# Two-layer gated cross-attention kernel: narrower top-k pieces, guard rows sent ahead of two key loads, and the second attention's first keys and queries loaded in the phase before

## The chip, the cores and the metric

One core of a Trainium2 chip runs the whole program in one launch. The metric is device time in microseconds of that core. The median of three runs of the kernel before is 3328.2 us (3325.5 to 3335.14).

## What is computed

The reference is a two-layer block over x (16 sequences of 256 tokens, 128 wide) and a context (16 x 1601 tokens, 96 wide), in float32:

```
x = x + tanh(g_xattn[0]) * L0_xattn(ln(x), ctx)   # 4 heads; top 32 of 1601 scores, softmax over them,
                                                  # mean over heads; FiLM, a long convolution, an MLP, a layer norm
x = x + tanh(g_ffn[0])   * L0_ffn(ln(x))          # 8 experts, one per token, at most 512 tokens each
x = x + tanh(g_xattn[1]) * L1_xattn(ln(x), ctx)
x = x + tanh(g_ffn[1])   * L1_ffn(ln(x))          # 8 experts, one per token, hidden 512

L1_xattn(x, c):  q = x @ w_q + b_q;  k = c @ w_k + b_k;  v = c @ w_v + b_v   # 16 heads of 8
                 w = softmax(q k^T / sqrt(8));  return (w v) @ w_o + b_o
```

The first attention needs, for each of 16 x 4 x 256 = 16384 score rows of 1601 values, the 32 largest.

## The kernel before

The program is a row of phases, each a block in which every engine has its own instruction stream and waits on semaphores. A block ends when all engines have ended it.

**First attention** (`attention0_phase`, about 190 to 1400 us). It walks 16 batches of 8 score tiles (4 heads x 2 halves of 128 rows). TensorE makes a tile of 128x1601 scores, ScalarE copies it to SBUF (`sc`, L870), VectorE finds the 32nd largest of each row, ScalarE and GpSimd turn that into masked exponentials (L877, L617, L883), VectorE adds tiles in pairs (L1044), TensorE multiplies them on. VectorE's search cuts a row into pieces of `PICK` = 51 columns (32 pieces), takes the eight largest of each (`MAX8`, L986), and then searches the 32 x 8 = 256 candidates with four `MAX8` (L1020) and three `MATCH_REPLACE8` (L1022). The first pass of the next tile is woven in: two pieces ahead of each step of the second search. If a row has more than eight of its top 32 in one piece, the candidates are not enough. ScalarE and TensorE count for each tile the values above the found threshold (`side`, `dps`, `doubts`); VectorE reads the count (`settle`, L974) and, where it is too high, searches the whole tile again with `select_all` (L961): four times `MAX8` and `MATCH_REPLACE8` over 1601 columns, and three passes more. ScalarE's exponential of that tile waits for `settled`.

**Convolution** (`conv_phase`), which also splits the keys of batches 0 and 1 into three bf16 parts (`keys` in DRAM), and the **middle phase** (`middle_phase`, 1485 to 1804 us): MLP, the first experts, and the queries of the second attention, split into three bf16 parts and saved by SyncE in 24 DMAs (L1322), three for each group of two batches. SyncE's order there is: eight loads of `FO` (from the third on each after `x_ready` of the group two before), 39 stores of a blank row block into `sorted` (L1318), the 24 saves. `x_ready` of a group says that `FO`, `Y` and `X0` of it have been read.

**Second attention** (`attention1_phase`, 1804 to about 3090 us). Scores must carry float32 precision through bf16 products, so rows of `ks` and `qs` hold seven pairs of parts (`PAIRS`, 7 x 8 = 56 rows) for even heads and, 64 rows further, for odd heads; three rows more, the guard rows, hold ones in `ks` and the parts of minus the row maximum in `qs`, so that a 59-row product (L1974) gives score minus maximum. Before them go 56-row products (L1949) of which VectorE takes only maxima (L2056). `ks[i]`, `qs[i]` and `va[i]` exist twice; batch b uses number b % 2.

At its start VectorE sets both `ks` to 1.0 (L2048) and adds the output bias to `X` (L2050, L2051); GpSimd sets both `qs` and both `va` to 0 (L1818, L1821). SyncE loads keys and queries of batches 0 and 1 only after that (`ready`, `ks_ready`), 28 DMAs per group of four heads. Then comes a prologue: maxima for batch 0 and the first head group of batch 1, 80 pieces of work; then 16 batches.

A batch has four head groups, a group 13 key tiles (`kt`). At each key tile TensorE does the scores of four heads, a product for maxima of the batch ahead, and the products with the values for the tile two before (L1987: four heads, each into its own 32 of the 128 output partitions, since `va` has `VW` = 32 columns per head, of which 9 carry something); ScalarE does the exponentials (L2030). In the last group, at the sixth and seventh key tile, TensorE turns the parts of the maxima (`guard`, L1953), VectorE copies them to `mT` (L2074), and SyncE sends `mT` to DRAM (L1901), waits for it, and loads it into the guard rows of the other `qs` (L1906). The first scores of the next batch wait for `guard_in`. Maxima run one batch ahead, those of the first head group two.

SyncE's order in the second attention (`batch(b)`, L1916) is what the change touches:

```
for g in range(HG - 1): load(b + 2, par, g, True)      # groups 0, 1, 2; each waits for pv_done of group g of batch b
load_values(b + 2, True)
guard(b + 1, 1 - par, ...)                             # waits for mT_ready
load(b + 2, par, HG - 1, True)                         # group 3
```

Each `load` is 14 DMAs of keys (L1887) and 14 of queries (L1888). The maxima of (b + 2, group 2) are due at group 1 of batch b + 1, those of group 3 at group 2. GpSimd meanwhile spreads the values into `va` (L1834) and splits later batches' keys (L1839 on).

**Second experts** (`mixture1_phase`), untouched.

Of the kernel before, what the change touches and what calls it, by code (L numbers as in the profile page):

```python
# [15 lines left out]
P = 128  # L16
# [15 lines left out]
BIG = 1e30  # L32
HIDDEN = 2.0 ** 45
# [3 lines left out]
PICK = 51  # L37
# [1164 lines left out]
def middle_phase(nc, a, k):  # L1202
# [3 lines left out]
    with ExitStack() as ctx:  # L1206
# [32 lines left out]
        blank = sb("m_blank", [P, ROW])  # L1239

# [60 lines left out]
        dve_step, pool_step, blank_ready, blanked = sem("m_dve_step"), sem("m_pool_step"), sem("m_blank_ready"), sem("m_blanked")  # L1301
        block = ctx.enter_context(nc.Block())

        @block.sync
        def _(sp):
            for name, t in (("g_ffn", gcol), ("b_ffn", bcol)):
                sp.dma_start(t[:, :], a["L0_xattn_" + name].unsqueeze(1)).then_inc(w_in, 16)
            for g in range(NG):
# [4 lines left out]
                if g == 1:  # L1313
                    for name, t in rowsb.items():
                        sp.dma_start(t[:, :], a["L0_xattn_" + name].partition_broadcast(P)).then_inc(rows_in, 16)
            sp.wait_ge(blank_ready, 1)
# [12 lines left out]
        def _(pool):  # L1329
# [3 lines left out]
            def constants():  # L1333
# [10 lines left out]
                pool.sem_inc(consts, 1)  # L1344
                st.link(g_.memset(blank[:, :], 0.0))
# [305 lines left out]
def attention1_phase(nc, a, k):  # L1651
# [8 lines left out]
    PAIRS = [(0, 0), (1, 0), (2, 0), (0, 1), (1, 1), (2, 1), (0, 2)]  # L1660
    ROWS = 64
    GUARD = DH1 * len(PAIRS)
# [7 lines left out]
    with ExitStack() as ctx:  # L1670
# [6 lines left out]
        ks = [sb(f"ks{i}", [P, H1 // 2, NK], BF16) for i in range(2)]  # L1677
        qs = [sb(f"qs{i}", [P, H1, S], BF16) for i in range(2)]
        vn = sb("vn", [P, KT, D])
        kfb = sb("kfb", [P, NK])  # L1680
        kpb = [sb(f"kpb{n}", [P, NK], BF16) for n in range(3)]
        va = [sb(f"va{i}", [P, KT, H1, VW]) for i in range(2)]
# [15 lines left out]
        ready, vn_in, va_ready = sem("a_ready"), sem("vn_in"), sem("va_ready")  # L1698
# [5 lines left out]
        pe_passed, pool_passed, ks_ready = sem("a_pe_passed"), sem("a_pool_passed"), sem("ks_ready")  # L1704
# [106 lines left out]
        def _(pool):  # L1811
# [13 lines left out]
            st.restart()  # L1825

# [30 lines left out]
            spread_values(1, 1)  # L1857
            for b in (2, 3):
                split_keys(b)
# [10 lines left out]
        def _(sp):  # L1870
# [3 lines left out]
            def load(b, par, g, started):  # L1874

                if started:
# [673 lines left out]
```

## Time and profile before

| | |
|---|---|
| profiled execution, its own time | 3325.87 us |
| its span, first to last instruction | 3324.4 us |
| median of three runs | 3328.2 us |
| TensorE busy (matmul) | 2556.5 us, 77% |
| VectorE busy | 2380.3 us, 72% |
| ScalarE busy | 2055.0 us, 62% |
| GpSimd busy | 1246.9 us, 38% |
| mean granted TensorE clock | 0.879 |
| L2056 maxima, VectorE, x1024 | 957.4 us, 988 ns each |
| L2030 exponentials, ScalarE, x1664 | 896.6 us |
| L986 pieces' `MAX8`, VectorE, x4096 | 562.9 us, 197 ns each |
| L1987 value products, TensorE, x6656 | 555.8 us, 407 ns each |

Busy time of a group counts overlap once, so a mean times a count can be more than it. Four products of L1987 into four output quarters overlap. A clock of 1.0 is 2.4 GHz, 0.5 is 1.2 GHz. A bracket behind an instruction in a timeline is the idle time of its engine before it, with what ended it.

### The profile page before, as it was taken

The page shows a single profiled execution, that of the slowest core. Times are in us where ns is not written, and L with a number is a line of the kernel's source. Part 1 is how long each engine was busy: PE and PEld are TensorE (multiplying, and loading weights), DVE is VectorE, ACT ScalarE, POOL GpSimd, SP SyncE. Part 2 cuts the span into 40 slices and gives each one's busy share as a digit, 9 for nine tenths or more (in the row PEclk, how much of TensorE's full clock was granted, in tenths as well). Part 3 has the DMA queues.
Part 4 walks back from the last instruction along what each step waited for, and adds up shares of the span by engine and source line. Part 5 has one row for each costly group of instructions (what it writes and reads, how often), then busy time and mean ns, then how long its engine had stood idle before and what let it go on. Part 6 is the DMA issues. An engine that isn't in the chain of part 4 may idle for free. (4 is left out here: it accounts for less than half of the span.)

```text
span 3324.4 us, 68050 instructions
## 1 busy us (share of the span) xinstructions
PE 2556.5 (77%) x19550; PEld 1303.9 (39%) x19550; DVE 2380.3 (72%) x7659; ACT 2055.0 (62%) x3368; POOL 1246.9 (38%) x1587
## 2 busy tenths in 40 slices
PE   1058888888678888758784589898989889999468
PEld 0035555555445555535321133333333333333335
DVE  5948887787887878636545988888888878883312
ACT  1148888888668888615221077777777777779112
POOL 2037766777557767613102032221111112100332
PEclk9978988898888888889787589999999999999679
DMA  2010010001001001083001633232322323220221
GB/s 54 0 31 32 32 42 33 31 31 50 30 18 46 31 31 42 26 274 95 1 18 29 102 97 89 86 90 81 84 82 84 85 87 85 81 53 2 71 77 45
DMA packets 136744, 195.94 MB, mean 59 GB/s; under 512 B 51842, under 2 KB 104511, under 8 KB 136363
## 3 DMA queue, kind: packets, MB, share of 16 engines
q1 hardware_dynamic: 126350, 152.17, 16.8%
q0 software_dynamic: 10016, 39.46, 3.3%
q8 instruction: 148, 2.42, 0.3%
q14 instruction: 230, 1.88, 0.2%
HBM read 125.38 MB, written 66.62 MB: 58 GB/s over the span
## 5 line engine op out<-in xcount | busy, mean ns | idle before, releaser
L2030 ACT ACTIVATE pb<-sps 128x512 f32<-128x512 f32 (+1 forms) x1664 | 896.6, 596 | 377.3 <-PE sps L1974 363.1
L2056 DVE TENSOR_REDUCE mx<-wps 128x2 f32<-128x802 f32 x1024 | 957.4, 988 | 157.0 <-PE wps L1949 140.7
L986 DVE MAX8 cand<-sc 128x8 f32<-128x51 f32 (+1 forms) x4096 | 562.9, 197 | 193.8 <-issue 162.0
L1987 PE MATMUL ops<-pb,va 128*32 128x256 f32 x6656 | 555.8, 407 | 7.6 <-ACT ot L2036 7.2
L749 PE MATMUL scores<-ctxT,qT 97*128 97x512 f32 (+1 forms) x1024 | 437.6, 576 | 43.8 <-ACT sc L870 42.7
L1949 PE MATMUL wps<-ks,qs 56*128 56x401 bf16 x2048 | 384.7, 361 | 105.1 <-DVE mx L2056 53.2
L1974 PE MATMUL sps<-qs,ks 59*128 59x256 bf16 (+1 forms) x3328 | 363.5, 284 | 70.3 <-DMA qs<-guards 69.8
L1834 POOL COPY va<-vn 128x128 f32<-128x128 f32 (+1 forms) x208 | 49.9, 292 | 796.6 <-PE ops L1987 720.0
L749 PEld LDWEIGHTS scores<-ctxT,qT 97*128 97x128 f32 x1024 | 210.5, 215 | 274.9 <-issue 220.6
L1974 PEld LDWEIGHTS sps<-qs,ks 59*128 59x128 bf16 (+1 forms) x3328 | 120.7, 96 | 411.0 <-ACT pb L2030 242.2
L617 POOL TENSOR_TENSOR prf<-sc,prf 128x1601 f32<-128x1601 f32 x64 | 230.0, 3594 | 119.0 <-ACT prf L877 118.1
L617 POOL TENSOR_TENSOR prs<-sc,prs 128x1601 f32<-128x1601 f32 x64 | 230.8, 3607 | 94.8 <-ACT prs L877 94.8
L1987 PEld LDWEIGHTS ops<-pb,va 128*32 128x32 f32 x6656 | 133.5, 110 | 213.1 <-issue 108.6
L723 PE MATMUL misc<-diag,prs 128*128 128x128 f32 (+1 forms) x1664 | 203.1, 280 | 9.3 <-DVE prs L1044 4.7
L891 ACT ACTIVATE side<-sc,below 128x1601 bf16<-128x1601 f32 x128 | 207.3, 1620 | 1.7 <-POOL below L611 1.7
L1949 PEld LDWEIGHTS wps<-ks,qs 56*128 56x128 bf16 x2048 | 110.6, 97 | 240.9 <-DVE mx L2056 165.3
L723 PEld LDWEIGHTS misc<-diag,prs 128*128 128x128 f32 (+1 forms) x1664 | 192.8, 191 | 11.1 <-DVE prs L1044 6.3
L870 ACT COPY sc<-scores 128x1601 f32<-128x1601 f32 x128 | 188.4, 1472 | 11.8 <-PE scores L749 11.8
L1020 DVE MAX8 top<-cleft 128x8 f32<-128x256 f32 x384 | 157.5, 410 | 0.1
L732 PE MATMUL misc<-prT,ctxn 128*96 128x128 f32 (+1 forms) x832 | 117.7, 308 | 45.7 <-ACT prT L851 45.7
L611 POOL TENSOR_SCALAR below<-slack,top 128x1 f32<-128x1 f32 x128 | 140.7, 1099 | 13.0
L732 PEld LDWEIGHTS misc<-prT,ctxn 128*96 128x96 f32 (+1 forms) x832 | 110.7, 189 | 52.5 <-ACT prT L851 52.5
(408 smaller groups left out, 3697.1 us busy)
## 6 DMA issues: line engine op xcount, KB each, us to landing
ks<-keys SPq DMA_DIRECT2D x896, 50.0 KB
keys<-kpb POOLq DMA_DIRECT2D x42, 400.2 KB, 3.3
toep<-kernpad SPq DMA_DIRECT2D x8, 2048.0 KB, 15.0
qs<-queries SPq DMA_DIRECT2D x896, 8.0 KB
values<-vs SPq DMA_DIRECT2D x16, 832.0 KB, 3.7
vn<-values SPq DMA_DIRECT2D x16, 832.0 KB, 4.7
keysf<-kf SPq DMA_DIRECT2D x16, 800.5 KB, 4.6
kfb<-keysf POOLq DMA_DIRECT2D x14, 800.5 KB, 5.5
```

The costliest lines, as they stand in the source:

```text
L617: g.tensor_tensor(pr[s][:, :], sc[s % 4][:, :], pr[s][:, :], ALU.subtract).then_inc(kept_ready, 1)
L723: ins = t.matmul(m[0:kn(kt), (kt % 4) * P:(kt % 4) * P + P], pr[s][:, kt * P:kt * P + kn(kt)], diag[s // 2][:, :], start=(p == 0), stop=(p ...
L732: ins = t.matmul(m[0:C, 0:P], ctxn[par][0:kn(kt), kt, :], prT[0:kn(kt), kt, :], start=(kt == 0), stop=(kt == KT - 1))
L749: ins = t.matmul(scores[:, c:c + n], q, ctxT[par][0:C + 1, c:c + n], start=True, stop=True)
L870: s_.copy(sc[s % 4][:, :], scores[:, 0:NK]).then_inc(scores_out, 1)
L891: s_.activation(side[s % 2][:, :], sc[s % 4][:, :], ACT.Sign, bias=below32[:, s % 2:s % 2 + 1], accum_out=sides[:, s % 2:s % 2 + 1]).then_ ...
L986: st.add(v.max(cand[s % 2][:, n, :], sc[s % 4][:, c:c + w]))
L1949: ins = t.matmul(buf[:, 512 * odd:512 * odd + WIN], qs[par][r, h + odd, q * P:q * P + P], ks[par][r, h // 2, (WIN - 1) * c:(WIN - 1) * c + ...
L1974: ins = t.matmul(sps[(UNITS * g + u) % SB][0:kn(kt), i, :], ks[par][r, h // 2, kt * P:kt * P + kn(kt)], qs[par][r, h, :], start=True, stop ...
L1987: ins = t.matmul(ops[VW * i:VW * i + VW, 0:S], va[par][0:kn(kt), kt, 4 * g + i, :], pb[(UNITS * g + 2 * kt + i % 2) % 8][0:kn(kt), i // 2, :],
L2030: nc.scalar.activation(pb[(UNITS * g + u) % 8][0:rows_, :, :], sps[(UNITS * g + u) % SB][0:rows_, :, :], ACT.Exp).then_inc(p_ready, 1)
L2056: v.tensor_reduce(mx4[:, q, h:h + 2, c], both, AX.X, ALU.max).then_inc(work_read, 1)
```

## The change

- `PICK` goes from 51 to 46: 35 pieces instead of 32, 280 candidates instead of 256.
- `PAIRS`, `ROWS`, `GUARD` move to the top of the file.
- `ks`, `qs`, `kfb`, `vn` of the second attention are no tensors of their own any more: they lie over `FO`, `X0` with `XF` (now one tensor), and `Y`, and so exist in the middle phase.
- SyncE loads all keys and all queries of batches 0 and 1 in the middle phase: keys and guard rows of ones in 32 DMAs after the last `x_ready`, ahead of the blank stores; queries in 28 DMAs after the second group's saves. The block ends only when they have landed.
- GpSimd sets a small tensor of ones (3 x 1601) for the guard rows. The whole memsets of `ks`, `qs` and `va` go; `va` has 9 columns per head and only its ninth is set.
- VectorE clears the PSUM bank `ops` once. The bias is added to `X` by GpSimd, after it spread the values of batches 0 and 1; VectorE's first guard copy waits for it.
- SyncE's order in a batch becomes: groups 0 and 1, values, guard, groups 2 and 3.

```diff
-PICK = 51
+PICK = 46
@@ middle_phase, sync
                 if g == 1:
                     for name, t in rowsb.items():
                         sp.dma_start(t[:, :], ...).then_inc(rows_in, 16)
+            sp.wait_ge(x_ready, NG)
+            sp.wait_ge(ones_ready, 1)
+            for b in range(2):
+                for odd in range(2):
+                    for i, (_, kp) in enumerate(PAIRS):
+                        r = slice(ROWS * odd + DH1 * i, ROWS * odd + DH1 * (i + 1))
+                        sp.dma_start(k.ks[b][r, :, :], kall[b, odd, kp]).then_inc(keys_in, 16)
+                    r = ROWS * odd + GUARD
+                    sp.dma_start(k.ks[b][r:r + 3, :, :], ones3[:, :].unsqueeze(1).to_broadcast([3, H1 // 2, NK])
+                                 ).then_inc(keys_in, 16)
             sp.wait_ge(blank_ready, 1)
...
             for g in range(NG):
                 sp.wait_ge(parts_ready, g + 1)
...
+                if g == 1:
+                    sp.wait_ge(saved[0], 48)
+                    for b in range(2):
+                        for odd in range(2):
+                            for i, (qp, _) in enumerate(PAIRS):
+                                r = slice(ROWS * odd + DH1 * i, ROWS * odd + DH1 * (i + 1))
+                                sp.dma_start(k.qs[b][r, odd:H1:2, :], qall[odd, qp, :, :, b * S:(b + 1) * S]
+                                             ).then_inc(queries_in, 16)
...
+            sp.wait_ge(keys_in, 16 * 2 * 2 * (len(PAIRS) + 1))
+            sp.wait_ge(queries_in, 16 * 2 * 2 * len(PAIRS))
@@ attention1_phase
-        va = [sb(f"va{i}", [P, KT, H1, VW]) for i in range(2)]
+        va = [sb(f"va{i}", [P, KT, H1, DH1 + 1]) for i in range(2)]
@@ gpsimd
-            for i in range(2):
-                st.link(g_.memset(qs[i][:, :, :], 0.0))
-                pool.sem_inc(ready, 1)
-            for i in range(2):
-                st.add(g_.memset(va[i][:, :, :, :], 0.0))
-            st.after()
...
             spread_values(0, 0)
             spread_values(1, 1)
+            st.link(g_.tensor_scalar(k.bo1[:, :], k.bo1[:, :], k.TG[:, 1:2], 0.0, ALU.mult, ALU.add))
+            st.link(g_.tensor_tensor(X[:, :, :], X[:, :, :], rows(k.bo1[:, :], T), ALU.add))
+            pool.sem_inc(biased, 1)
@@ sync
             for b in range(2):
-                sp.wait_ge(ready, b + 1)
-                sp.wait_ge(ks_ready, b + 1)
-                for g in range(HG):
-                    load(b, b, g, False)
                 load_values(b, b == 1)
             guard(0, 0, False)
 
             def batch(b, par):
 
-                for g in range(HG - 1):
-                    load(b + 2, par, g, True)
+                for g in range(HG - 2):
+                    load(b + 2, par, g)
                 load_values(b + 2, True)
                 guard(b + 1, 1 - par, not (isinstance(b, int) and b == 0))
-                load(b + 2, par, HG - 1, True)
+                for g in range(HG - 2, HG):
+                    load(b + 2, par, g)
@@ tensor, maxima
-                if opens:
-                    pe.wait_ge(kq_in[par][h // 4], 16 * 2 * 2 * len(PAIRS) * visit)
+                if opens and not (isinstance(visit, int) and visit == 1):
+                    pe.wait_ge(kq_in[par][h // 4], 16 * 2 * 2 * len(PAIRS) * (visit - 1))
@@ tensor, values
-                    ins = t.matmul(ops[VW * i:VW * i + VW, 0:S], va[par][0:kn(kt), kt, 4 * g + i, :],
+                    ins = t.matmul(ops[VW * i:VW * i + DH1 + 1, 0:S], va[par][0:kn(kt), kt, 4 * g + i, :],
@@ vector
-            for i in range(2):
-                st.link(v.memset(ks[i][:, :, :], 1.0))
-                dve.sem_inc(ks_ready, 1)
-            st.link(v.tensor_scalar(k.bo1[:, :], k.bo1[:, :], k.TG[:, 1:2], None, ALU.mult))
-            st.link(v.tensor_tensor(X[:, :, :], X[:, :, :], rows(k.bo1[:, :], T), ALU.add))
+            st.link(v.memset(ops[:, :], 0.0))
+            dve.sem_inc(ops_blank, 1)
```

## Rows read from the trace of the kernel before

**Rows 1.** Waits of the whole span: engine line <- releaser: us in total, times, longest.

```profile
PE sps L1974 <- DMA qs<-guards: 69.8, 15, 6.6
```

**Rows 2.** Timeline of a batch's end: VectorE, SyncE's queue, TensorE.

```profile
2424.85 0.20 DVE L2074 COPY mT<-wps 48x128 bf16<-48x128 bf16 x1
...
2416.88 0.28 SPq L1887 DMA_DIRECT2D ks<-keys  x1
...
2428.85 0.28 SPq L1888 DMA_DIRECT2D qs<-queries  x1
2429.31 0.36 SPq L1893 DMA_DIRECT2D vn<-values  x1
2429.88 0.34 SPq L1901 DMA_DIRECT2D guards<-mT  x1
2435.22 0.58 SPq L1906 DMA_DIRECT2D qs<-guards  x2
...
2437.78 0.61 PE L1974 MATMUL sps<-qs,ks 59*128 59x256 bf16 x4 [5.71 <-DMA qs<-guards]
```

**Rows 3.** Timeline of the last batch boundary, and the windows row of that stretch.

```profile
3024.87 0.22 DVE L2074 COPY mT<-wps 48x128 bf16<-48x128 bf16 x1 [0.84 <-PE wps L1958]
...
3026.74 0.57 SPq L1906 DMA_DIRECT2D qs<-guards  x2
...
3030.86 0.27 PE L1974 MATMUL sps<-qs,ks 59*128 59x256 bf16 x1
...
3000.00:3050.00 50.00, 48.37 (x580) 17.46 (x572) 20.99 (x32) 46.16 (x92) 0.00 (x0) 1.00 0.01 3
```

**Rows 4.** Windows of L1987 on TensorE (busy, count, clock), then of all TensorE.

```profile
2388.00:2401.00 13.00, 7.03 (x88) 1.00 0.31 88
...
2437.70:2444.40 6.70, 3.35 (x28) 0.51 0.08 20
...
1982.90:2964.40 981.50, 881.87 (x9984) 0.94 0.30 84
```

**Rows 5.** Windows: stretch, length, busy PE, PEld, DVE, ACT, POOL; PEclk, DMA share, GB/s.

```profile
400.00:700.00 300.00, 254.24 (x1310) 171.28 (x1309) 242.66 (x1466) 253.73 (x349) 213.93 (x265) 0.90 0.10 35
```

**Rows 6.** Timeline of the second attention's start.

```profile
1806.56 10.73 DVE L2048 MEMSET ks<- 128x12808 bf16 x1 [6.14 <-issue]
...
1835.80 14.49 DVE L2056 TENSOR_REDUCE mx<-wps 128x2 f32<-128x802 f32 x16
```

**Rows 7.** Middle phase: line 1371's instructions; SyncE's queue.

```profile
L1371 DVE TENSOR_TENSOR xt<-xt,X x8: 691/693/693, 1492.2 to 1584.1; 128x512 f32<-128x512 f32 x8
...
1556.95 20.36 SPq L1318 DMA_DIRECT2D sorted<-m_blank  x39
1683.29 118.53 SPq L1322 DMA_DIRECT2D queries<-q_p  x24
```

**Rows 8.** Instructions of line 1135, products with 16 columns of weights.

```profile
L1135 PE MATMUL cv<-toep,xc x256: 376/379/634, 1433.8 to 1481.2; 128*16 128x256 f32 x128
```

**Rows 9.** Instructions of line 968: durations ns min/median/max, first and last start.

```profile
L968 DVE MAX8 top<-sc x8: 1829/1829/1830, 837.4 to 963.6; 128x8 f32<-128x1601 f32 x8
```

**Rows 10.** Timeline of GpSimd at three batch starts (start us, duration us, engine, line).

```profile
566.24 0.40 POOL L591 COPY xn<-X 128x256 f32 x1
...
781.17 0.40 POOL L591 COPY xn<-X 128x256 f32 x1
...
1029.60 0.40 POOL L591 COPY xn<-X 128x256 f32 x1
```

**Rows 11.** Timeline of VectorE in one tile's search.

```profile
718.62 0.41 DVE L1020 MAX8 top<-cleft 128x8 f32<-128x256 f32 x1
718.95 2.10 DVE L986 MAX8 cand<-sc 128x8 f32<-128x51 f32 x18
```

**Rows 12.** Timeline where ScalarE follows GpSimd's threshold most closely.

```profile
665.25 0.19 POOL L601 TENSOR_SCALAR negm<-top 128x1 f32<-128x1 f32 x1
...
666.57 1.63 ACT L877 ACTIVATE prf<-sc,cutoff 128x1601 f32<-128x1601 f32 x1
```

More of the change, by code:

```diff
@@ L32 @@
 BIG = 1e30
+PAIRS = [(0, 0), (1, 0), (2, 0), (0, 1), (1, 1), (2, 1), (0, 2)]
+ROWS = 64
+GUARD = DH1 * len(PAIRS)
 HIDDEN = 2.0 ** 45
@@ L1315, in _ @@
                         sp.dma_start(t[:, :], a["L0_xattn_" + name].partition_broadcast(P)).then_inc(rows_in, 16)
+            sp.wait_ge(x_ready, NG)
+            sp.wait_ge(ones_ready, 1)
+            kall = k.keys.rearrange("b n (pr o d) c -> b o n d pr c", o=2, d=DH1)
+            qall = k.queries.rearrange("n (pr o d) c -> o n d pr c", o=2, d=DH1)
+            for b in range(2):
[6 more added lines that the diff above has]
+                                 ).then_inc(keys_in, 16)
             sp.wait_ge(blank_ready, 1)
@@ L1344, in constants @@
                 pool.sem_inc(consts, 1)
+                st.link(g_.memset(ones3[:, :], 1.0))
+                pool.sem_inc(ones_ready, 1)
                 st.link(g_.memset(blank[:, :], 0.0))
@@ L1675, in sem @@
             return ctx.enter_context(nc.semaphore(name))
[L1677 to L1680, printed above, removed]
+        ks, qs, vn, kfb = k.ks, k.qs, k.vn, k.kfb
         kpb = [sb(f"kpb{n}", [P, NK], BF16) for n in range(3)]
-        va = [sb(f"va{i}", [P, KT, H1, VW]) for i in range(2)]
+        va = [sb(f"va{i}", [P, KT, H1, DH1 + 1]) for i in range(2)]
         pb = [sb(f"pb{i}", [P, 2, S]) for i in range(8)]
@@ L1696, in attention1_phase @@
         X, ident = k.X, k.ident
-        ready, vn_in, va_ready = sem("a_ready"), sem("vn_in"), sem("va_ready")
+        vn_in, va_ready, ops_blank, biased = sem("vn_in"), sem("va_ready"), sem("ops_blank"), sem("a_biased")
         kq_in = [[sem(f"kq_in{i}{g}") for g in range(HG)] for i in range(2)]
@@ L1872, in _, with load @@
             qall = k.queries.rearrange("n (pr o d) c -> o n d pr c", o=2, d=DH1)
[L1874 to L1880 removed]
+            def load(b, par, g):
+                sp.wait_ge(pv_done, KT * (HG * (b - 2) + g + 1))
+                sp.sem_inc(sp_passed, 1)
+                sp.wait_ge(k.keys_out, 48 * (b - 1))
+                sp.sem_inc(sp_passed, 1)
                 pr = slice(2 * g, 2 * g + 2)
@@ L1955, in guard @@
                 pe.wait_ge(mparts_ready, b + 1)
+                if isinstance(b, int) and b == 0:
+                    pe.wait_ge(identb_ready, 1)
                 work(job)
@@ L1984, in values @@
                     pe.wait_ge(ops_read, HG * b + g)
+                if kt == 0 and first and g == 0:
+                    pe.wait_ge(ops_blank, 1)
                 pe.wait_ge(p_ready, UNITS * HG * b + UNITS * g + 2 * kt + 2)
                 for i in range(4):
-                    ins = t.matmul(ops[VW * i:VW * i + VW, 0:S], va[par][0:kn(kt), kt, 4 * g + i, :],
+                    ins = t.matmul(ops[VW * i:VW * i + DH1 + 1, 0:S], va[par][0:kn(kt), kt, 4 * g + i, :],
                                    pb[(UNITS * g + 2 * kt + i % 2) % 8][0:kn(kt), i // 2, :],
@@ L2073, in guard @@
                     dve.wait_ge(mT_saved, 16 * b)
+                if isinstance(b, int) and b == 0 and q == 0:
+                    dve.wait_ge(biased, 1)
                 st.link(v.tensor_copy(mT[:, q, :], buf[0:3 * H1, 0:P // 2].bitcast(BF16)))
@@ L2521, in flamingo_kernel @@
                 conv_phase(nc, a, k)
+                flat = [t.rearrange("p a d -> p (a d)") for t in
+                        (k.FO[:, :, :], XX[:, :, :, :].rearrange("p i t d -> p (i t) d"), k.Y[:, :, :])]
+                words = H1 // 2 * NK // 2
+                k.ks = [t[:, 0:words].bitcast(BF16).rearrange("p (r c) -> p r c", c=NK) for t in flat[0:2]]
+                k.kfb = flat[0][:, words:words + NK]
+                k.vn = flat[1][:, words:words + KT * D].rearrange("p (t d) -> p t d", d=D)
+                k.qs = [flat[2][:, i * H1 * S // 2:(i + 1) * H1 * S // 2].bitcast(BF16).rearrange("p (h c) -> p h c", c=S)
+                        for i in range(2)]
                 middle_phase(nc, a, k)
-        attention1_phase(nc, a, k)
+                attention1_phase(nc, a, k)
         mixture1_phase(nc, a, k)
```

17 lines of the change are left out of this document (7 added, 10 removed).

## The prediction

> **What bounds the kernel now.** I read the waits of the whole run first, then the timelines at two kinds of batch boundary of the second attention, the windows with the granted clock, and last the first attention's tiles. The profiled execution took 3325.87 us, 2.3 below the median of 3328.2; the sum is made against the 3325.9.
>
> The second attention runs on TensorE and VectorE together (88 value products in 13 us are 11 key tiles at 8 a tile, 1.18 us each and 15.4 us for a group of 13 [rows 4]), except at its batch boundaries: there TensorE waits for the guard rows, 15 times, 69.8 us in all [rows 1]. One boundary shows why [rows 2]. VectorE has `mT` ready at 2425.05. SyncE is then still issuing the 28 loads of group 2 (2416.88 to 2429.13), issues 832 KB of values, sends `mT` only at 2429.88, has it back at 2435.22 and loads the guard rows; TensorE starts at 2437.78 after 5.71 us idle, so it wanted them at 2432.07. At the last boundary no loads are left [rows 3]: `mT` ready at 3025.09, second DMA at 3026.74, TensorE goes on at 3030.86 with no wait at all and the clock stays at full speed (1.00).
>
> The wait costs more than itself. After it, TensorE's granted clock is 0.51 for 6.7 us, the lower level of 1.2 GHz; before, it was 1.00 [rows 4]. In the low stretch 28 value products start in 6.7 us (4.18 per us) against 88 in 13 us (6.77 per us): 38% of that time is lost. Over 13 batches the mean clock is 0.94, so 12% of 981.5 us, 118 us, are at the low level.
>
> The first attention is ScalarE's: 253.7 us busy in 300, VectorE 242.7 [rows 5]. VectorE has some slack there, except where a tile is searched again.
>
> **The change part by part.**
>
> *Guards ahead of groups 2 and 3.* SyncE is free from group 1's loads on. At the last boundary it needs 1.65 us from `mT` ready to the guard DMA [rows 3]; the guard load itself takes 2.56 us (2435.22 to 2437.78, [rows 2]). So the guard rows are there at 2425.05 + 1.65 + 2.56 = 2429.3, 2.8 us before they are wanted. The values load is now ahead of the guard by 11 us and has landed. The first of the 15 waits, 4.5 us, is the prologue's and stays; it has no loads ahead of it. The other 14 go: 69.8 - 4.5 = 65.3 us. What is late next: nothing at TensorE's order; VectorE has 64 maxima a batch of 957.4/1024 = 0.935 us busy (line 2056 in the table), 60 us, and a few us of small work, while the batch falls from 75.5 (981.5/13) to about 68 us. It is the next bound, but not yet reached.
>
> *The low clock after it.* At 14 boundaries the low stretch ends 6.4 to 9.3 us after the wait does, by the granted clock, 7.6 in the mean; 14 x 7.6 x 0.38 = 40.6, 41 us. One of them stands in [rows 4], and [rows 3] has the boundary without a wait and without a fall. Bounds: 0, if the small products at a batch's start make the fall, to 118 x 0.5 = 59 us. I take 41.
>
> The Trainium skill gives another price for such a stretch (TensorE: Matmul & The Clock Gate, section Terms): the time at the lower level times the share of pulses taken away, so a half here. By that the 118 us would cost 59 and the sum would come out 18 us lower (rival 6). The row does not agree, 38% and not 50% [rows 4].
>
> *Keys of groups 2 and 3 later.* Group 2's loads start after the guard's, at 2427.3 instead of 2416.88, need 12.3 us to issue [rows 2] and end at 2439.6; group 3's follow to 2452. TensorE needs group 2 one group into the next batch, 2432 + 15.4 and some 3 us of the last batch's output work, 2450.5, and group 3 at 2466. With a few us to land (the 832 KB, the guard and back took 8 us together in [rows 2]) some 5 us are left for the first and more for the second. Cost 0; above it, see the slow rival.
>
> *The start.* Today the first maxima reduction is at 1835.80 [rows 6], behind 10.7 us of memset, 15 us of loads and the bias on `X`. Now VectorE begins at 1806.56 as before with a PSUM memset of 512 columns (the memset of 12808 bf16 columns took 10.73 us, so under 1 us), and everything else is in place: 1807.3. Gain 28.5 us, all on the path, since the 80 pieces of the prologue follow one another on VectorE. GpSimd's bias add and its spreading have until the first guard copy, 80 x 14.49/16 = 72.5 us later: hidden. Bounds 25 to 31.
>
> *Middle phase.* `x_ready` of the last group comes at about 1585 [rows 7]. The loads of [rows 2] brought 0.8 MB in 13 us, 62 GB/s with the issuing engine as the limit; 5.7 MB of keys take at most 92 us, to 1677; the blank stores, 20 us by their row, then end at 1697, at worst 14 us after the first query save was due (1683.29). The eight groups' saves come 118.5/7 = 16.9 us apart and each buffer is wanted again only two groups later, 34 us, so this is hidden; the queries' 28 loads (0.9 MB) fall into the gap after group 1. Cost 0, at worst 10 us at the end of the block. GpSimd's small memset lies beside TensorE's first MLP group: 0, at most its own us or two.
>
> *Nine columns.* Value products with 16 columns of weights and 256 moving take 379 ns and also four at a time [rows 8], those with 32 columns 403: no change, bounds -10 to +10 us.
>
> *Pieces.* The eight `MAX8` of 1601 columns [rows 9] mean that two tiles were searched again. Their price is in [rows 10]: three batches from 566.24 to 781.17 take 214.9 us, the three with the two tiles (to 1029.60) 248.4; 33.5 us for two. Which rows have more than eight of their top 32 in one piece can be counted from the reference's inputs (seed 0): with pieces of 51, one row in each of two tiles (batch 8, head 0 and batch 9, head 3), which agrees with the rows' place in the trace; with 46, none. So 33.5 us go. Against it: 18 `MAX8` of 51 take 2.10 us, 117 ns each [rows 11]. From 256 to 1601 columns `MAX8` grows by 1.055 ns a column (410 to 1829 ns), so one of 46 takes 111.5: 35 x 111.5 - 32 x 117 = 160 ns. The second search has seven steps over 24 columns more, 177 ns. Together 0.34 us a tile, 43 us of VectorE for 128 tiles. Where ScalarE comes closest behind, it takes the tile 1.1 us after GpSimd's threshold [rows 12]; the threshold itself moves by 0.1 us in its own tile (16 shorter pieces lie ahead of it), and VectorE is idle 57 us in 300 [rows 5], 1.7 us a tile (a batch of 8 tiles takes 71.6) against 0.34 added, so the lag stays under that 1.1. Cost 0; if the cover is gone, 43.
>
> **Sum.** 3325.9 - 65.3 - 41 - 28.5 - 33.5 = 3157.6; I say 3158.
>
> **The rivals.**
> 1. The low clock stays at the boundaries. For it: in some of the 14 the fall begins only as the wait ends, and the short transposing products come there anyway. Against: [rows 3]. 3158 + 41 = 3199.
> 2. Pieces exposed: VectorE becomes the first attention's bound. For: 81% busy; against: it idles while ScalarE works. 3158 + 43 = 3201.
> 3. Guards are still late by half. For: 2.8 us of margin rests on one undisturbed trip; against: nothing else is in the queue. 14 x 2.3 = 32, and the low clock with it: 3158 + 32 + 41 = 3231.
> 4. Slower: the keys come late. Where groups 2 and 3 together miss their group, TensorE waits in every batch at the place where it has no wait today. The margin is about 5 us; each us past it costs 14. The gain of 168 us is used up at 12 us of waiting a batch, 17 us later than reckoned. For: both loads are now back to back, 24 us of issue, beside 2 MB of GpSimd's. With 14 us a batch, 3158 + 196 = 3354.
> 5. The change doesn't do what it says: the start is not earlier, because SyncE's new work ends the middle phase later. 3158 + 28 = 3186.
> 6. The low clock costs half of all its time, 118 x 0.5 = 59 us instead of 41. For: whatever stands behind TensorE slows with it; against: 38% by the counts of [rows 4], VectorE's reduction does not slow with TensorE, and some of the low time lies inside waits that are counted already. 3158 - 18 = 3140. (The skill's price above.)
>
> **How the numbers follow.** The forecast has 0.62 (its own range 3142 to 3180), rival 1 0.12, rival 2 0.06, rival 3 0.07, rival 4 0.03, rival 5 0.04, rival 6 0.06. The range 3132 to 3210 takes in rivals 1, 2, 5 and 6 and leaves out 3 and 4. What a measurement of this kernel can tell from no change is 0.3%, 10 us: faster 0.96, same 0.01, slower 0.03.
>
> **What would show it.** Right: no wait of `sps` for `qs<-guards` but the first; the batches' mean clock near 1.0 with 68 us a batch; first reduction at 1807; no `MAX8` over 1601 columns; the first attention ending some 33 us earlier. Wrong: waits of `wps` for `ks` or `qs` at groups 1 and 2; ScalarE waiting for GpSimd's threshold; a middle phase that ends later than 1804 less those 33.

## The result, and the profile after

The kernel after takes 3189.53 us (median of four runs, 3186.89 to 3194.58), the kernel before, in the same comparison, 3331.67 (3325.5 to 3337.04). The ratio is 0.9576, 95% interval 0.9553 to 0.9598. That is inside the predicted range and 31 us above the 3158 forecast. The profiled execution took 3194.58 us, 131.3 less than the one before. By stages, from the starts and ends of the tiles named, in us of the two profiled executions:

| stage | before | after | difference | forecast |
|---|---|---|---|---|
| to the first score copy `sc` | 207.9 | 210.4 | +2.5 | 0 |
| first attention, to the last `side` | 1186.9 | 1155.7 | -31.2 | -33.5 |
| convolution and middle phase, to the first maxima reduction | 441.0 | 408.8 | -32.2 | -28.5 |
| prologue of the second attention | 79.3 | 78.9 | -0.3 | 0 |
| its 16 batches, first to last exponential | 1171.6 | 1101.3 | -70.3 | -106.3 |
| the rest | 237.7 | 238.0 | +0.3 | 0 |

So 36 of the missing 37 us are missing in the 16 batches. The page of the kernel after: busy times, the granted clock by slices, and the groups that answer to the table of before (`maxima` is now line 2078, the exponentials line 2055, the value products line 2012, the pieces line 990).

```profile
PE 2533.8 (79%) x19550; PEld 1274.0 (40%) x19550; DVE 2360.1 (74%) x8010; ACT 2050.6 (64%) x3368; POOL 1241.8 (39%) x1586
...
PEclk9978988989999899778878589999999999999589
...
L2055 ACT ACTIVATE pb<-sps 128x512 f32<-128x512 f32 (+1 forms) x1664 | 894.0, 596 | 282.5 <-PE sps L1997 268.8
L2078 DVE TENSOR_REDUCE mx<-wps 128x2 f32<-128x802 f32 x1024 | 954.1, 989 | 93.1 <-PE wps L1970 77.7
L990 DVE MAX8 cand<-sc 128x8 f32<-128x46 f32 (+1 forms) x4480 | 587.0, 194 | 164.8 <-issue 128.6
L2012 PE MATMUL ops<-pb,va 128*9 128x256 f32 x6656 | 527.2, 389 | 9.4 <-ACT ot L2061 8.4
```

**The waits that answer to [rows 1]**, second attention of the kernel after (us in all, times, longest):

```profile
PE sps L1997 <- issue: 19.8, 5, 4.3
PE sps L1997 <- DMA Y<-guards: 4.0, 1, 4.0
```

The guard waits are gone but for the prologue's. In their place stand five pauses for which the view names no releaser ("issue": the engine waited for nothing that the profile shows). They come at the ends of batches 2, 4, 6, 8 and 10 and nowhere else. The timeline of one of them answers to [rows 2]; the bracket is TensorE's idle time:

```profile
2189.75 0.21 DVE L2098 COPY mT<-wps 48x128 bf16<-48x128 bf16 x1
...
2190.14 0.34 SPq L1924 DMA_DIRECT2D guards<-mT  x1
2191.58 0.59 SPq L1929 DMA_DIRECT2D Y<-guards  x2
2192.94 0.29 SPq L1910 DMA_DIRECT2D FO<-keys  x1
...
2200.93 0.61 PE L1997 MATMUL sps<-Y,XX 59*128 59x256 bf16 x4 [4.01 <-issue]
```

and the same place one batch earlier, where SyncE issues the same loads, TensorE does not stop and the scores follow 5.3 us behind the guard load. Above, 5.3 us behind it is 2196.9, which is where TensorE's idle time begins:

```profile
2120.79 0.21 DVE L2098 COPY mT<-wps 48x128 bf16<-48x128 bf16 x1
2121.18 0.34 SPq L1924 DMA_DIRECT2D guards<-mT  x1
...
2122.62 0.59 SPq L1929 DMA_DIRECT2D Y<-guards  x2
...
2127.89 0.60 PE L1997 MATMUL sps<-Y,FO 59*128 59x256 bf16 x4
```

What differs is the code. Batches 1 to 12 are a loop of six passes of two batches (`walk`, line 1822 after, 1797 before), so behind batches 2, 4, 6, 8 and 10 TensorE, ScalarE and VectorE jump back (SyncE and GpSimd have loops of their own); behind batch 12 they fall through, and there is no pause. The trace has the loop's own instructions, seen by their line: kind, number, shortest, median and longest in ns, first and last start. "PEldq" is TensorE's sequencer. Kernel after, then the kernel before:

```profile
L1822 ACTq COMPARE_BRANCH  x6: 40/45/50, 2051.7 to 2769.8; - x6
L1822 PEldq COMPARE_BRANCH  x6: 83/4331/4737, 2051.7 to 2769.8; - x6
```

```profile
L1797 PEldq COMPARE_BRANCH  x6: 83/5870/6167, 2127.7 to 2885.5; - x6
```

A jump back of TensorE takes 4.0 to 4.7 us (the five single records), the last one, not taken, 83 ns. Before, it took 5.5 to 6.2 us and lay in the same stretch as the guard wait: at the boundary of [rows 2] it ran from 2431.3 to 2437.1, while the guard rows came at 2437.8. The cover was the wait that the change removes.

**Clock and pace of the batches**, windows of the kernel after: all of value products in a full-speed stretch and in the stretch behind a jump (they answer to [rows 4]), then batches 1 to 12 whole. Columns as in [rows 5]; the first two rows are of line 2012 alone.

```profile
2388.00:2401.00 13.00, 6.46 (x88) 1.19 (x80) 1.00 0.38 118
2344.90:2351.60 6.70, 3.42 (x28) 0.50 (x32) 0.50 0.27 72
```

```profile
1917.80:2771.00 853.20, 796.47 (x9218) 269.58 (x9216) 754.79 (x913) 682.29 (x1296) 197.28 (x264) 0.96 0.33 91
```

88 products in 13 us and 28 in 6.7, as before: the low level costs the same 38%. Batches 1 to 12 take 71.1 us each (853.2/12), not 68, at a clock of 0.96; low stretches within the batches fell from 137 to 69 us. Of the 69, 51 are five stretches of 10.2 us at the jumps, 4 lie in batch 0, and 14 are four short ones of 3.4 us (from 2182.2, 2325.5, 2544.0 and 2755.6), 15 to 20 us ahead of a batch's end. Two of these four ends, those of batches 9 and 12, have no jump.

**Start of the second attention** (answers to [rows 6]) and the middle phase (to [rows 7]: instructions of line 1402, which was 1371, then SyncE's queue):

```profile
1774.16 0.48 DVE L2072 MEMSET ops<- 128x512 f32 x1 [3.62 <-PEq L1210]
...
1774.79 2.79 DVE L2078 TENSOR_REDUCE mx<-wps 128x2 f32<-128x802 f32 x3
```

```profile
L1402 DVE TENSOR_TENSOR xt<-xt,XX x8: 691/691/694, 1462.5 to 1554.4; 128x512 f32<-128x512 f32 x8
```

```profile
1593.86 16.73 SPq L1331 DMA_DIRECT2D XX<-keys  x7
1610.63 1.83 SPq L1333 DMA_DIRECT2D XX<-m_ones  x1
1612.51 33.48 SPq L1337 DMA_DIRECT2D sorted<-m_blank  x39
1653.57 21.21 SPq L1341 DMA_DIRECT2D queries<-q_p  x6
1674.82 9.76 SPq L1349 DMA_DIRECT2D Y<-queries  x28
1693.44 78.49 SPq L1341 DMA_DIRECT2D queries<-q_p  x18
```

**First attention** (answers to [rows 10]); three batches now take 215.0 and 212.6 us:

```profile
573.04 0.40 POOL L595 COPY xn<-XX 128x256 f32 x1
...
788.01 0.40 POOL L595 COPY xn<-XX 128x256 f32 x1
...
1000.65 0.40 POOL L595 COPY xn<-XX 128x256 f32 x1
```

### The profile page after: what moved, and what is told of

Read it like the earlier page. It is cut to its first block and busy times, and to the rows that moved or that the text cites. A ratio compares the mean times of both kernels' runs of the same rounds, so it can differ in the third digit from the quotient of the medians.

```text
span 3193.1 us, 68227 instructions
## 1 busy us (share of the span) xinstructions
PE 2533.8 (79%) x19550; PEld 1274.0 (40%) x19550; DVE 2360.1 (74%) x8010; ACT 2050.6 (64%) x3368; POOL 1241.8 (39%) x1586
## 5 line engine op out<-in xcount | busy, mean ns | idle before, releaser
L990 DVE MAX8 cand<-sc 128x8 f32<-128x46 f32 (+1 forms) x4480 | 587.0, 194 | 164.8 <-issue 128.6
L2012 PE MATMUL ops<-pb,va 128*9 128x256 f32 x6656 | 527.2, 389 | 9.4 <-ACT ot L2061 8.4
L1854 POOL COPY va<-XX 128x128 f32<-128x128 f32 (+1 forms) x208 | 50.3, 295 | 706.4 <-PE ops L2012 698.7
L1970 PE MATMUL wps<-FO,Y 56*128 56x401 bf16 x1024 | 196.8, 368 | 49.4 <-DVE mx L2078 34.6
L1970 PE MATMUL wps<-XX,Y 56*128 56x401 bf16 x1024 | 186.6, 343 | 26.4 <-DVE mx L2078 18.1
L1997 PE MATMUL sps<-Y,XX 59*128 59x256 bf16 (+1 forms) x1664 | 184.9, 282 | 20.0 <-issue 19.8
L1997 PE MATMUL sps<-Y,FO 59*128 59x256 bf16 (+1 forms) x1664 | 180.3, 278 | 4.3 <-DMA Y<-guards 4.0
L2012 PEld LDWEIGHTS ops<-pb,va 128*9 128x9 f32 x6656 | 99.1, 88 | 208.2 <-issue 98.4
L1024 DVE MAX8 top<-cleft 128x8 f32<-128x280 f32 x384 | 167.7, 437 | 0.1
L1997 PEld LDWEIGHTS sps<-Y,XX 59*128 59x128 bf16 (+1 forms) x1664 | 63.1, 96 | 197.9 <-ACT pb L2055 124.5
## 6 DMA issues: line engine op xcount, KB each, us to landing
toep<-kernpad SPq DMA_DIRECT2D x8, 2048.0 KB, 14.9
```

What stands on the lines that cost most here:

```text
L990: st.add(v.max(cand[s % 2][:, n, :], sc[s % 4][:, c:c + w]))
L1024: link(v.max(tp[:, 8 * r:8 * r + 8], x))
L1970: ins = t.matmul(buf[:, 512 * odd:512 * odd + WIN], qs[par][r, h + odd, q * P:q * P + P], ks[par][r, h // 2, (WIN - 1) * c:(WIN - 1) * c + ...
L1997: ins = t.matmul(sps[(UNITS * g + u) % SB][0:kn(kt), i, :], ks[par][r, h // 2, kt * P:kt * P + kn(kt)], qs[par][r, h, :], start=True, stop ...
L2012: ins = t.matmul(ops[VW * i:VW * i + DH1 + 1, 0:S], va[par][0:kn(kt), kt, 4 * g + i, :], pb[(UNITS * g + 2 * kt + i % 2) % 8][0:kn(kt), i ...
```

## Experiments

Eleven kernels. The ratio of each is to the kernel before, timed beside it, with the 95% interval.

### The loop written out for three engines (`a_unroll`) and for TensorE alone (`a_unroll_pe`)

```diff
@@ attention1_phase, walk
-            with eng.Fori(0, (B - 4) // 2) as i:
+            for i in range((B - 4) // 2):
                 batch(2 * i + 1, 1, {1: i + 2, 2: i + 2}, False, 2)
                 batch(2 * i + 2, 0, {1: i + 2, 2: i + 3}, False, 2)
```

> The kernel after, with the second attention's loop over batches 1 to 12 (six passes of two batches) written out for TensorE, ScalarE and VectorE; SyncE and GpSimd keep their loops. Theory J (the jump back): at the ends of batches 2, 4, 6, 8 and 10 the engines jump back to the loop's start, and TensorE's branch takes 4.0 to 4.7 us there; that is what the pauses of 3.6 to 4.4 us before the first scores of batches 3, 5, 7, 9, 11 are (19.8 us), and the fall of the clock behind each (10.2 us of low level, 38% of it lost, 3.9 us each) comes from them. Written out: 5 x (4.0 + 3.9) = 39 us less, 3150 us, no pause at a batch boundary, batches of 68 us all through. Rival G (the guard rows are still late every second batch, because group 2's loads are issued right behind them): the pauses stay where they are, 3185 to 3190 us. Rival C (the clock falls at these places whatever TensorE waits for): the pauses go, the low stretches stay, 3170 us.

Measured: 3139.63 us, ratio 0.9427 (0.9389 to 0.9465), 50 us less than the kernel after. Waits of `sps` in the batches are gone, and every batch from 1 to 13 takes 66.43 or 66.44 us at full clock (the window is batches 1 to 12):

```profile
1926.30:2723.50 797.20, 756.11 (x9219) 252.73 (x9216) 750.32 (x913) 679.37 (x1296) 197.24 (x264) 1.00 0.35 97
```

Theory J holds, G and C fall: SyncE's order and its DMAs are the same, and in batches 1 to 15 neither pause nor low stretch is left. The gain is 11 us larger than expected. A batch inside the loop that neither jumps nor loses clock takes 67.61 us, written out 66.43: 1.18 us, 14 in twelve batches, and the expectation had the number and left it out of its sum. What differs in such a batch is the sequencers' register arithmetic for semaphore values: in batch 1 of the kernel after the trace has 177 `ALU_OP` on TensorE's sequencer, 153 on ScalarE's and 68 on VectorE's, and written out none.

> The kernel after, with the same loop written out for TensorE alone; ScalarE and VectorE still jump back. Between their last instruction before the jump and the first behind it ScalarE shows 3.6 us and VectorE 3.8 us too. Theory J with all engines alike: TensorE's pause goes, but ScalarE comes back only some 2.5 us after it would be wanted, so TensorE stands behind it for 1 to 2.5 us instead of 4: 5 x 1.5 to 3 us less and the clock partly held, 3170 to 3182 us. Rival T (only TensorE's jump matters, the others jump while they would idle anyway): as when all are written out, 3150 us. Rival G: 3185 to 3190 us.

Measured, with only `walk(pe, ...)` written out: 3171.79 us, ratio 0.9533 (0.9496 to 0.9569), 18 us less than the kernel after by the medians and 14 by the ratios, inside J's 3170 to 3182. The timeline at the end of batch 4: ScalarE and VectorE come 2 us late from their own jumps, and TensorE stands 1.3 us behind them.

```profile
2196.18 2.14 ACT L2060 ACTIVATE pb<-sps 128x512 f32<-128x512 f32 x4 [2.05 <-PE ops L2017]
...
2196.84 0.49 PE L2002 MATMUL sps<-Y,XX 59*128 59x256 bf16 x3 [1.32 <-ACT pb L2060]
2197.18 1.89 DVE L2083 TENSOR_REDUCE mx<-wps 128x2 f32<-128x802 f32 x2 [2.03 <-issue]
```

The five stops are 1.2 to 1.7 us long; after three of them the clock still fell, for 6.8 us each. Their branches read 45 and 63 ns, yet these engines pause too: the branch's own duration shows the cost on TensorE only. This run also says whose register arithmetic costs time. TensorE has none left here, and the undisturbed batches 9, 11 and 12 still take 67.75 us, so the 1.18 us belong to ScalarE's or VectorE's; which of the two was not tried.

### Two jumps instead of five (`a_double`)

```diff
-            with eng.Fori(0, (B - 4) // 2) as i:
-                batch(2 * i + 1, 1, {1: i + 2, 2: i + 2}, False, 2)
-                batch(2 * i + 2, 0, {1: i + 2, 2: i + 3}, False, 2)
+            with eng.Fori(0, (B - 4) // 4) as i:
+                for j in range(2):
+                    batch(4 * i + 2 * j + 1, 1, {1: 2 * i + j + 2, 2: 2 * i + j + 2}, False, 2)
+                    batch(4 * i + 2 * j + 2, 0, {1: 2 * i + j + 2, 2: 2 * i + j + 3}, False, 2)
```

> The kernel after with the second attention's loop of six passes of two batches turned into three passes of four: two jumps back instead of five, all in the same loop arithmetic on registers. It parts the 50 us that writing the loop out brought (3139.6 against 3189.5) into jumps and registers. Theory J: a jump costs 4.0 us of pause and 3.9 of clock, and the registers' part, 1.2 us a batch (67.6 us for a batch in the loop at full clock, 66.4 for one written out), stays: 3 x 7.9 = 24 us less, 3166 us, pauses only at the ends of batches 4 and 8. Rival R: the gain was the registers', the pauses are covered elsewhere: 3185 to 3190 us. Rival L: a longer body makes a jump dearer, 10 us and more each, since more must be fetched: 3175 to 3185 us.

Measured: 3168.44 us, ratio 0.9520 (0.9488 to 0.9551), 21 us less than the kernel after by the medians, 19 by the ratios. The waits of `sps` and the branch:

```profile
PE sps L1998 <- issue: 6.2, 2, 3.1
```

```profile
L1822 PEldq COMPARE_BRANCH  x3: 83/3577/3583, 2191.4 to 2745.8; - x3
```

Batches 1 to 12 take 826.2 us. Twelve at 67.61 would be 811.3, so 14.9 us are above that here, and 42 in the kernel after. That parts the 56.1 us between 853.3 and the 797.2 of the written-out loop: 42 for jumps and lost clock (19.8 of them pauses), 14 for registers. Not all of the 42 is the jumps'. This trace, too, has short low stretches ahead of a batch's end, in batches 2, 8 and 12; batches 2 and 12, which do not begin behind a jump, take 69.02 and 68.89 us, so one costs about 1.35. By that estimate (14.9 - 3 x 1.35)/2 = 5.4 us stay for a jump here and (42 - 4 x 1.35)/5 = 7.3 in the kernel after. The five versions of the kernel after in which TensorE's loop is written out have no such stretch, but neither has `b_order`, which keeps it; what makes them was not tried. R and L fall: a longer body's jump was no dearer.

### The kernel before with the loop written out (`b_unroll`) and with the new order alone (`b_order`)

The edit of `b_unroll` is that of `a_unroll`.

> The kernel before, with the same loop written out for TensorE, ScalarE and VectorE. Its boundaries behind even batches wait 5.1 to 6.6 us, those behind odd batches 3.8 to 4.4, and TensorE's branch takes 5.5 to 6.2 us in the former, at the same time as the wait for the guard rows. Theory J: branch and guard wait lie over each other, so writing it out brings only the difference, 5 x 1.3 = 6.5 us, 3322 us against 3328, and the low stretches stay. Rival A (the two add up, the branch is paid in full): 5 x 4 = 20 us less, 3308 us.

Measured: 3305.38 us, ratio 0.9938 (0.9917 to 0.9959), 21 us less. By the time alone rival A would have won. The trace says otherwise:

```profile
PE sps L1974 <- DMA qs<-guards: 62.7, 15, 6.0
```

The waits fall by 7.1 us only (69.8 in [rows 1]), as J says for jumps under guard waits, and the low stretches stay at 138 us. Batches 1 to 12 are 16.9 us shorter (908.1 to 891.2). The waits at their ends fell by 9.2 us (the prologue's wait, outside them, was 1.5 longer); the other 8 fit the registers' part, which this expectation left out too, but no run shows them by themselves.

```diff
@@ SyncE, batch(b)
-                for g in range(HG - 1):
+                for g in range(HG - 2):
                     load(b + 2, par, g, True)
                 load_values(b + 2, True)
                 guard(b + 1, 1 - par, not (isinstance(b, int) and b == 0))
-                load(b + 2, par, HG - 1, True)
+                for g in range(HG - 2, HG):
+                    load(b + 2, par, g, True)
```

> The kernel before with only SyncE's new order in a batch (groups 0 and 1, values, guard rows, groups 2 and 3). The prediction on record has 65.3 us for the waits and 41 for the clock, 106 together: 3222 us. Theory J: the five jumps back stand uncovered once the guard rows are in time, so 65.3 - 19.8 = 45.5 us of waits and, with 64 us less at the low level, 24.5 us of clock go: 70 us, 3258 us. If the order alone brought over 100 us, the jump would have to be the fault of another part of the change.

Measured: 3263.24 us, ratio 0.9817 (0.9781 to 0.9854), 61 us less than before by that ratio, 67 by the batches of the trace (1171.6 to 1104.2). The order alone uncovers the same five pauses, and it also makes the jumps shorter, 4.5 to 5.1 us against the 5.5 to 6.2 of the kernel before:

```profile
PE sps L1975 <- issue: 21.9, 5, 4.6
PE sps L1975 <- DMA qs<-guards: 4.9, 1, 4.9
```

### The other parts of the change, each taken back from the kernel after (`a_pick51`, `a_va32`, `a_start_only`)

```diff
-PICK = 46
+PICK = 51
```

> The kernel after with pieces of 51 columns again (32 instead of 35, 256 candidates instead of 280). Theory: the two tiles that are searched again come back with 33.5 us, and the 43 us less work of VectorE (0.34 us a tile) bring nothing, because it is hidden: 3189.5 + 33.5 = 3223 us. Rival: the longer search is exposed (in the first attention's last batch the kernel after lost some 6 us against the kernel before): then some 6 to 43 us of the 33.5 are given back, 3217 down to 3180 us. With narrow pieces the first attention's batches took 71.8 us; they should take the same here.

Measured: 3226.06 us, ratio 0.9682 (0.9657 to 0.9707), 35 us more than the kernel after (0.0106 of 3329). The batches with the two tiles take 88.6 and 87.3 us in the profile, against 69.8 and 71.8. The longer second search is not exposed. What looked like it, the last batch at 91.2 us against 85.1, comes with either width: 85 to 86 us (from its first `sc` to the last `side`) in `before`, `a_start_only` (51), `a_unroll`, `a_unroll_both` (46) and `a_long0` (48), 91 to 92 in the kernel after, `a_pick51`, `b_order` and the others.

```diff
-        va = [sb(f"va{i}", [P, KT, H1, DH1 + 1]) for i in range(2)]
+        va = [sb(f"va{i}", [P, KT, H1, VW]) for i in range(2)]
...
+                st.add(g_.memset(va[i][:, :, :, :], 0.0))
...
-                    ins = t.matmul(ops[VW * i:VW * i + DH1 + 1, 0:S], va[par][0:kn(kt), kt, 4 * g + i, :],
+                    ins = t.matmul(ops[VW * i:VW * i + VW, 0:S], va[par][0:kn(kt), kt, 4 * g + i, :],
```

> The kernel after with va of 32 columns a head again, set to zero as a whole at the start, and 32 output partitions a product. The prediction on record has 0 for the nine columns, bounds -10 to +10. Theory: a product takes 403 to 407 ns instead of 389, TensorE is ahead of its consumers for most of a batch, and the batches at full clock show 66.8 against 66.4 us, 0.4 each: 6 us more, 3196 us; GpSimd's two memsets (11 us) are hidden behind VectorE's 72 us of prologue. Rival: TensorE is the bound inside a group and pays the full 14 ns x 1664 x 4 / 4 = 23 us: 3212 us.

Measured: 3205.93 us, ratio 0.9616 (0.9588 to 0.9645); the intervals of this and of the kernel after touch, the medians are 13 to 16 us apart. In the traces batches 1 to 12 take 854.2 against 853.3, all 16 3.1 us more, and the prologue 4.7 more, which stands in rows: GpSimd's work, pushed back by its memsets, now runs beside VectorE's small steps on the maxima.

```profile
1850.02 3.63 DVE L2090 CAST mparts<-mneg 128x32 bf16<-128x32 f32 x1
1850.38 3.23 POOL L1876 TENSOR_TENSOR FO<-FO,kpb 128x1601 f32<-128x1601 f32 x1
```

The same cast takes 0.18 us elsewhere (3.45 more), and a subtraction just ahead of it took 1.39 instead of 0.19: together 4.65. The remaining 5 to 8 us of the difference are not settled: the first attention, which this edit does not touch, took 7 us longer in this trace.

> The kernel after with pieces of 51 columns and SyncE's old order in a batch, so that of the change only the earlier loads, the memsets that are gone, the bias on GpSimd and the nine columns are left. Theory: the traces show the first reduction 31 us earlier against the middle phase's last work, the nine columns bring 6, the rest nothing: 3328 - 37 = 3291 us. Rival (the middle phase pays for the loads): 3300 to 3320 us, and the middle phase is longer than in the kernel before.

The edit is `PICK = 51` and SyncE's old order, both from above. Measured: 3287.37 us, ratio 0.9860 (0.9830 to 0.9891), 47 us less than before, interval 36 to 57; 37 were expected. No sign of a longer middle phase: the stretch to the first reduction is 403.2 us against 441.0.

### Both loops written out, other widths, and a longer body in the first attention

`a_unroll_both` has the first attention's loop, line 541, written out as well.

> The kernel after with both attentions' loops written out, the first attention's for all five engines' walks, the second's for TensorE, ScalarE and VectorE. The second alone gave 3139.6 us. The first attention's loop has 1354 TensorE instructions a pass and its jumps take 0.22 us, the second's 3449 and 4 to 4.7 us. Theory J: a body that the engine can hold jumps back for nothing, so only what the registers cost (1.2 us a batch in the second attention) is to be had: 14 x 0 to 1 us, 3125 to 3140 us. Rival: the first attention's low clock stretches hang on its jumps, 3100 to 3120 us.

Measured: 3139.59 us, ratio 0.9432 (0.9403 to 0.9460), the same as `a_unroll`. Theory J's upper end; the first attention has nothing of this kind to give, though VectorE's sequencer stands for 3.1 to 3.2 us behind each of its six taken jumps in the kernel after.

`a_unroll48` is `a_unroll` with `PICK = 48`.

> The kernel after with the second attention's loop written out (3139.6 us) and pieces of 48 columns instead of 46 (34 pieces, 272 candidates). No row has more than eight of its top 32 in a piece of 48, so no tile is searched again. Theory: VectorE has 0.1 us a tile less, which is hidden in the first attention: 3139.6 us within 0.3%. Rival: the first attention pays for pieces: down to 3130 us.

Measured: 3135.88 us, ratio 0.9429 (0.9401 to 0.9457): the same, as the theory says. It is among the fastest versions here, with `a_unroll`, `a_unroll_both` and the next one, whose intervals overlap: 5.7% under the kernel before and 1.5% under the kernel after.

`a_long0` is `a_unroll48` with this edit:

```diff
@@ attention0_phase, walk
-            with eng.Fori(0, (B - 2) // 2) as i:
-                step(2 * i + 1, 1, i + 2, False, False)
-                step(2 * i + 2, 0, i + 2, False, False)
+            with eng.Fori(0, 3) as i:
+                step(4 * i + 1, 1, 2 * i + 2, False, False)
+                step(4 * i + 2, 0, 2 * i + 2, False, False)
+                step(4 * i + 3, 1, 2 * i + 3, False, False)
+                step(4 * i + 4, 0, 2 * i + 3, False, False)
+            step(13, 1, 8, False, False)
+            step(14, 0, 8, False, False)
```

> The kernel of the last run (second attention's loop written out, pieces of 48; 3135.9 us) with the first attention's loop of seven passes of two batches turned into three passes of four, and two batches written behind it. It asks what makes a jump back dear. A pass then has 2708 TensorE instructions instead of 1354; the passes that cost 4 us in the second attention had 3449. Theory S (the size of the body decides, and 2708 is already too much): TensorE's branch takes 3.5 us and more instead of 0.22, twice. The time hardly moves, since ScalarE sets the first attention's pace: 2 x 0 to 4 us more, 3136 to 3144 us. Rival K (it is not the size, but what stands around the jump in the second attention): the branch stays at 0.22 us, time as before within 0.3%.

Measured: 3137.69 us, ratio 0.9421 (0.9388 to 0.9454), no change in time. The branch, in the kernel after (seven passes of two batches) and here (three passes of four):

```profile
L541 PEldq COMPARE_BRANCH  x7: 83/215/246, 425.2 to 1285.8; - x7
```

```profile
L541 PEldq COMPARE_BRANCH  x3: 82/4466/4659, 564.7 to 1144.9; - x3
```

Theory S holds: the same code, in a body twice as long, jumps back in 4.5 to 4.7 us instead of 0.22. ScalarE and GpSimd show it too. From their branch to their sequencer's next instruction it was 0.24 to 0.31 us with 308 and 242 instructions a pass, and is 2.4 to 2.5 and 2.7 to 3.4 us with 614 and 480. The time did not change, so the first attention does not pay for it.

## Why the forecast came out 31 us too low

- **Guard waits, the step that failed.** "The other 14 go: 65.3 us" was right about the guard rows: none is waited for. But the step took the whole idle time for the guards' and left out what TensorE itself does there. At five of the 14 boundaries it jumps back, 5.5 to 6.2 us of branch under the wait. Net 45.5 us went (65.3 - 19.8). The evidence was in the trace before: the waits at these five are 5.1 to 6.6 us, the other nine 2.9 to 4.7, and the boundary that was read as the proof that the clock does not fall without a wait [rows 3] has no jump. "So it wanted them at 2432.07" was wrong for the same reason: TensorE was in its branch until 2437.1.
- **The low clock after it.** The price was right (38%), the number of places wrong. A jump's pause lowers the clock as the guard wait did, and four short stretches, 14 us, stand apart from the jumps. Low time within the batches fell by 68 us, 26 at 38%, where 41 were forecast (14 stretches of 7.6 us, 106 us of low time). Rival 1 named this end (the low level stays) but with another cause and at all 14 boundaries. Written out, no low stretch is left in batches 1 to 15.
- **Sum of the two.** 106.3 forecast, 70.3 measured; `b_order` has it alone with 61 to 67.
- **Keys of groups 2 and 3.** Right: no wait of `wps` for them in any trace.
- **The start.** 28.5 forecast; from the first VectorE instruction to the first reduction 29.24 us became 0.63, 28.6. Another 2.5 came because VectorE enters the phase 3.6 instead of 6.1 us after its last work. With the phases before it the stretch is 32.2 shorter.
- **Middle phase.** Right at 0 for the end (its last query cast came 29.9 us earlier, its first `xt` sum 29.7). The blank stores ended at 1646 and not at 1697 of the worst case.
- **Nine columns.** 0 forecast, 3 us in the batches by the traces, and 13 to 16 together with the memsets by the measured times, of which 5 to 8 are not accounted for.
- **Pieces.** 33.5 forecast, 35 measured; no `MAX8` over 1601 columns is left. Had the 43 us of extra VectorE work (an estimate of the prediction) been exposed, `a_pick51` would not have been slower at all; they are hidden. Rival 2 falls.
- **First attention.** 6 us of its gain were hidden in this profile by a last batch of 91.2 us (clock 0.79 in 1275 to 1339, against 0.97 in its counterpart). The kernel after and `a_unroll` run the same code here and show 91.2 and 86.2 us, and both lengths occur with either width, so the width is not the cause; what is was not tried.

The convolution and middle phase gained 3.7 us more than forecast and the part up to the last `side` 4.8 less. These about cancel, so the error is the uncovered jump.

## What to carry to other kernels

Before a wait's whole time is booked as gain, look at what the waiting engine's sequencer does in the same microseconds: a loop's jump can hide there, and one boundary of each kind (jump, no jump) has to be read. If an engine's loop body is long, count its instructions and look at its branch in the trace, at the duration on TensorE and at the time to the sequencer's next instruction on the others; writing the loop out was worth 50 us here, 14 of them for another reason than the jump. When one part of a wait's cause goes, the clock that fell with it comes back only where nothing else stops TensorE.

## What the hardware showed that was not expected

- TensorE's branch back is cheap for a short body and takes microseconds for a long one, but does not grow further with the length. A pass had 1254 matmuls and weight loads (0.22 us), 2504 (4.5 to 4.7), 3072 (4.0 to 4.7) and 6144 (3.6); with the sequencer's own instructions in the trace these are 1359, 2712, 3448 and 6893. The Trainium skill (Runtime: NRT & Kernel Launch, section Instruction fetch mechanics) gives TensorE's instruction memory as 2048 instructions and says that a taken branch whose target isn't in the current two-page window waits for a fetch. The four bodies agree with a limit at 2048 and not with one at two pages of its 256 instructions, which all four exceed.
- The trace shows such fetches. Its instruction queues are `q8`, packets of 16 KB, and `q14`, packets of 8 KB. In the six short passes of the kernel after (426 to 1285 us) `q8` moves nothing and only `q14` is listed; in the two long ones of `a_long0` (564.7 to 1144.9) and in the second attention of the kernel after (2051.7 to 2769.8) it moves 13 and 16 packets a pass. Queue, packets, MB and share of the 16 engines' time, one line for each of the three stretches:

```profile
q14 instruction: 72, 0.59, 0.2%
...
q8 instruction: 26, 0.43, 0.3%
...
q8 instruction: 80, 1.31, 0.8%
```

- `q8` is not named as TensorE's in the trace; it follows the length of TensorE's pass. Behind each long branch of TensorE one or two of its packets start before TensorE goes on. That the engine waits for them is the reading that fits all runs.
- The Trainium skill's figure of about 108 ns for compare-and-branch (Advanced Engine Details and Errata, section Control Flow Timing) was met by no branch of TensorE here: 83 ns not taken, 207 to 247 taken back over a short body, 3.6 us and more over a long one.
- The same jump over 3072 took 5.5 to 6.2 us in the kernel before and 4.5 to 5.1 with SyncE's new order alone (`b_order`). In `a_start_only`, with the old order, it took 5.2 to 6.7. So its length depends on what SyncE issues in that stretch. The first `q8` packet starts 1.4 to 2.1 us behind the branch in the kernel before and 0.5 to 1.1 us in `b_order`; what holds it up was not tried.
- ScalarE and VectorE pause as well: 3.6 to 4.2 and 3.8 to 4.1 us in the kernel after from the branch to the sequencer's next instruction, with branches of 45 and 63 ns in the trace. With TensorE's loop alone written out (`a_unroll_pe`) it was 2.6 to 3.1 and 3.0 to 3.6, and TensorE stood 1.2 to 1.7 us. ScalarE's pass has 642 instructions in the trace, VectorE's 318, so the counts that part short from long on TensorE do not carry over.
- A batch inside the loop takes 1.18 us more than the 66.43 of one written out, without a jump or lost clock. Register arithmetic for semaphore values is what differs, and it is not TensorE's.
- Beside a GpSimd `TENSOR_TENSOR` of 3.23 us a VectorE cast of 0.18 us lasted 3.63.
- The first attention of kernels with pieces of 46 and 48, in eight traces, took 1153.5 to 1167.0 us with 245 to 304 us at the low level: among them 1155.7 and 1167.0 (the kernel after and `a_unroll`) for the same code: so two traces can differ by 10 us here with no cause in this part of the code.
